# Down products with the weights stationary, and VectorE in place of TensorE for the transposes of the expert part

## What is computed

```python
# attention: q from the normalised x, k and v from ctx_1024
qh, kh = rope(q @ wq.T), rope(k @ wk.T)          # 16 heads of 64
scores = where((j <= i) & (j >= i - 64), qh @ kh.T / 8, -1e30)
x = x + tanh(g_xattn) * (softmax(scores) @ vh) @ wo.T
# experts: xt is the normalised x, 2048 tokens
shared = sum over 2 of gelu(xt @ up.T) @ down.T
probs = softmax(xt @ router_w.T)                 # 16 experts
gate = probs where among the 4 largest, else 0
routed = sum over 16 of (gelu(xt @ up.T) * gate) @ down.T   # inner width 128
x = x + tanh(g_ffn) * (shared + routed)
```

## Time and profile before

| | |
|---|---|
| median of 3 runs | 535.76 us (534.08 to 537.0) |
| the profiled execution: own time, span | 533.94 us, 532.2 us |
| granted clock of PE, mean over the span | 0.996 of full |
| attention with the last heads, up to expert 4 | 0 to 322.8 us |
| experts 4 to 71 | 322.8 to 528.6 us |
| busy share PE, DVE, ACT, POOL | 97%, 64%, 59%, 51% |

### The profile page before, as it was taken

How to read it: one execution, slowest core, us unless ns; L and a number is a source line. 1 busy time by engine, 2 the same in 40 slices (tenths; PEclk the granted TensorE clock), 3 DMA queues, 4 the chain that set the end, 5 groups by cost and what they waited for, 6 DMA issues and landing times.

```text
span 532.2 us, 13189 instructions
## 1 busy us (share of the span) xinstructions
PE 514.6 (97%) x4904; PEld 454.5 (85%) x4904; DVE 343.2 (64%) x1122; ACT 311.7 (59%) x861; POOL 273.8 (51%) x212
## 2 busy tenths in 40 slices
PE   8788999999999999999999999999999999999997
PEld 5577797789889988888889789989999989999996
DVE  5768867658675687668766647665656465645444
ACT  3367667475766567765776665664456445544442
POOL 3899998779887978897998325430100010000000
PEclk9999999999999999999999899999999999999999
DMA  8262224011031101220221047205400540046001
GB/s 264 84 174 60 67 66 139 18 36 38 10 106 36 38 1 37 57 57 22 56 58 55 3 136 249 93 1 178 181 1 1 177 182 1 1 125 234 1 1 39
DMA packets 21614, 41.03 MB, mean 77 GB/s; under 512 B 3056, under 2 KB 5360, under 8 KB 21552
## 3 DMA queue, kind: packets, MB, share of 16 engines
q1 hardware_dynamic: 21552, 40.20, 24.5%
HBM read 30.62 MB, written 2.23 MB: 62 GB/s over the span
## 4 chain that ended last, share of the span: by engine, by line
PE 74%; POOL 9%; DVE 7%; issue 5%; ACT 3%; DMA 1%; SPq 0%; DVEq 0%; POOLq 0%; ACTq 0%
PE ring L934 51%; PE psS L934 9%; PE psO L1135 4%; PE psS L1104 4%; PE psT L1116 4%; POOL arena L433 2%; POOL prob L439 2%; POOL arena L435 2%; DVE arena L717 2%; POOL arena L426 1%; PE psT L1081 1%; POOL wl L447 1%; DVE wl L788 1%; DVE arena L720 1%; DVE arena L843 1%
## 5 line engine op out<-in xcount | busy, mean ns | idle before, releaser
L934 PE MATMUL ring<-xTh,wh 128*128 128x512 f32 x272 | 111.2, 409 | 3.2 <-DVE arena L720 2.9
L934 PE MATMUL ring<-xTl,wh 128*128 128x512 f32 x272 | 106.9, 393 | 0.0
L934 PE MATMUL ring<-xTh,wl 128*128 128x512 f32 x272 | 106.9, 393 | 0.0
L934 PE MATMUL ring<-wh,oTh 128*128 128x256 f32 x272 | 78.4, 288 | 2.0 <-POOL wl L447 0.8
L934 PE MATMUL ring<-wh,oTl 128*128 128x256 f32 x272 | 76.7, 282 | 0.0
L934 PE MATMUL ring<-wl,oTh 128*128 128x256 f32 x272 | 76.4, 281 | 0.0
L439 POOL TENSOR_TENSOR prob<-prob,rinv 128x512 f32<-128x512 f32 x64 | 68.0, 1063 | 16.3 <-DVE rinv L853 16.1
L775 DVE TENSOR_TENSOR oTl<-prob,oTh 128x512 fp32r<-128x512 f32 x64 | 45.4, 710 | 43.5 <-ACT oTh L531 43.3
L531 ACT ACTIVATE oTh<-prob 128x512 fp32r<-128x512 f32 x64 | 40.4, 631 | 55.5 <-PE ring L934 25.2
L515 ACT ACTIVATE sneg<-ring 128x512 f32<-128x512 f32 x72 | 42.9, 596 | 36.8 <-PE ring L934 36.2
L767 DVE TENSOR_TENSOR prob<-sneg,arena 128x512 f32<-128x512 f32 x64 | 47.4, 740 | 26.4 <-ACT sneg L515 26.4
(11 more groups left out here) (118 smaller groups left out, 1243.7 us busy)
## 6 DMA issues: line engine op xcount, KB each, us to landing
arena<-gate_scratch SPq DMA_DIRECT2D x64, 256.0 KB, 6.3
raw<-in_e SPq DMA_DIRECT2D x18, 256.0 KB, 2.6
raw<-in_w SPq DMA_DIRECT2D x16, 256.0 KB, 3.3
arena<-arena SPq DMA_DIRECT2D x16, 256.0 KB, 3.1
arena<-arena SPq DMA_DIRECT2D x16, 192.0 KB, 3.4
out<-x SPq DMA_DIRECT2D x16, 128.0 KB, 5.8
x<-in_x SPq DMA_DIRECT2D x3, 512.0 KB, 4.1
craw<-in_ctx SPq DMA_DIRECT2D x3, 512.0 KB, 5.2
```

The source lines that it names most:

```text
L934: last = pe.matmul(out, a, b, start=start and i == 0 and j == 0, stop=stop and i == n - 1 and j == 2, skip_group_check=check)
```

## The change

- `down` keeps the weights stationary and moves the 512 tokens: 6 matmuls of 512 columns in place of 12 of 256. The sums are then turned, 2 x 128 of the 256 values on partitions and 512 tokens along them, and so are z and the output tensor (the host turns it back).
- z needs x (after attention) turned too. DVE makes this copy, x1T, in four quarters per batch ("back" at e = 9, 12, 16, 17). A quarter is four transposes from 32 partitions, 256 values each, to the four groups of 32 partitions.
- In the expert part the normalised x of the next batch is turned by DVE as well ("turn", four quarters at e = 5 to 8), in place of PE's 8 transposes; rounding is "xhi" at 9 (ACT) and the remainder "xlo" at 10 (DVE). Batch 0's is still turned by PE.
- The router's product has its weights stationary (4 matmuls of 512 columns) and DVE turns the logits (4 transposes) and the gates (4 transposes) for all batches. PE's transposes of gates go.
- "stat" goes to e = 3, "norm_a" and "norm_b" both to 4, "r", "rexp", "pick_a", "pick_b" one later (11 to 14).
- In the last heads, ACT's copy of head 58 comes before the exponential of head 60; behind it PE, ACT and DVE have another order.

```diff
-            for e, kind in ((4, "stat"), (6, "norm_a"), (7, "norm_b"), (9, "xT"), (10, "r"), (11, "rexp"),
-                            (12, "pick_a"), (13, "pick_b"), (15, "gT")):
+            for e, kind in ((3, "stat"), (4, "norm_a"), (4, "norm_b")):
+                after[b * NE + e].append((kind, B + b + 1))
+            for quarter in range(4):
+                after[b * NE + 5 + quarter].append(("turn", 4 * (b + 1) + quarter))
+            for e, kind in ((9, "xhi"), (10, "xlo"), (11, "r"), (12, "rexp"), (13, "pick_a"), (14, "pick_b"),
+                            (15, "gT")):
+                after[b * NE + e].append((kind, b + 1))
...
+            for quarter, e in enumerate((9, 12, 16, 17)):
+                after[b * NE + e].append(("back", 4 * b + quarter))
...
+            def turn(dst, src, a):
+                blocks = src[QUAD * a:QUAD * (a + 1), :, :].rearrange("p t (k c j) -> p t k c j", k=KC, c=4)
+                for c in range(4):
+                    to = dst[QUAD * c:QUAD * (c + 1), :, :].rearrange("p k (t a j) -> p t k a j", t=TT, a=4)
+                    last = dve.transpose(to[:, :, :, a, :], blocks[:, :, :, c, :])
+                return last
...
+                by_tokens = banks(("r", b))[0][0:QUAD, :].rearrange("p (t a j) -> p t a j", t=TT, a=4)
+                for a in range(4):
+                    last = dve.transpose(logits[QUAD * a:QUAD * (a + 1), :, :], by_tokens[:, :, a, :])
...
+                elif kind == "turn":
+                    b, a = divmod(n, 4)
+                    dve.wait_ge(ln_norm, B + b + 1)
+                    turn(xnT, xn, a).then_inc(xn_turned, 1)
+                elif kind == "back":
+                    b, a = divmod(n, 4)
+                    dve.wait_ge(y_out, GROUPS * (b + 1))
+                    turn(x1T, x[:, b, :, :], a).then_inc(x1_turned, 1)
...
-                for t in range(TT):
-                    half, at = t // 2, (t % 2) * D
-                    last = product(sums(b, half)[:, at:at + D],
-                                   [(hi[:, t * P:(t + 1) * P], lo[:, t * P:(t + 1) * P])],
-                                   [cols(i, D, D)], start=(e == 0 and t % 2 == 0), stop=(e == NE - 1),
-                                   check=True)
-                    last.then_inc(down_pe, 1)
+                for kc in range(KC):
+                    product(sums(b, kc), [cols(i, D + kc * P, P)], [gated_parts(n)], start=e == 0,
+                            stop=e == NE - 1, check=True).then_inc(down_pe, 1)
```

The last heads on PE, before and after:

```diff
             transpose_probs(60)
             expert(0)
+            transpose_probs(61)
             do(("y", UNITS - 2))
-            do(("gT", 0))
-            transpose_probs(61)
-            expert(1)
             values(30)
             transpose_probs(62)
+            expert(1)
+            transpose_probs(63)
             expert(2)
-            transpose_probs(63)
+            values(31)
             down(0)
-            values(31)
             expert(3)
```

More of the change, by code:

```diff
@@ L369, in store @@
             def store(b):
-                for t in range(TT):
-                    sp.wait_ge(z_out, TT * b + t + 1)
-                    sp.dma_start(out_d[b][:, t, :], x[:, b, t, :]).then_inc(out_done, 16)
+                for i in range(4):
+                    part = slice(i % 2 * (L // 2), (i % 2 + 1) * (L // 2))
+                    sp.wait_ge(z_out, 4 * b + i + 1)
+                    sp.dma_start(out_d[b][:, i // 2, part], z_of(b)[:, i // 2, part]).then_inc(out_done, 16)
             def do(job):
@@ L828, in do @@
                 elif kind == "z":
[L829 to L832, removed]
+                    dve.wait_ge(x1_turned, 4 * (n + 1))
+                    for i in range(4):
+                        kc, part = i // 2, slice(i % 2 * (L // 2), (i % 2 + 1) * (L // 2))
+                        dve.wait_ge(down_pe, KC * (NE * (n + 1) - 1) + kc + 1)
+                        dve.scalar_tensor_tensor(z_of(n)[:, kc, part], sums(n, kc)[:, part],
+                                                 tg[:, 1:2], x1T[:, kc, part],
                                                  ALU.mult, ALU.add).then_inc(z_out, 1)
@@ L1076, in do @@
                     X = side(B + n)
-                    for t in range(TT):
-                        for kc in range(KC):
-                            for part in (xTh[X], xTl[X]):
-                                last = pe.matmul(two[0][:, t * 2 * NR:(t + 1) * 2 * NR],
-                                                 part[:, kc, t * P:(t + 1) * P],
-                                                 rw_parts[:, kc, :, :].rearrange("p a e -> p (a e)"),
-                                                 start=kc == 0 and part is xTh[X],
-                                                 stop=kc == KC - 1 and part is xTl[X])
-                    last.then_inc(r_pe, 1)
-                elif kind == "gT":
-                    pe.wait_ge(r_gate, n + 1)
-                    for t in range(TT):
-                        last = pe.transpose(two[0][0:NR, t * P:(t + 1) * P], gate[:, t, :], ident[:, :])
-                    last.then_inc(gT_pe, 1)
+                    for kc in range(KC):
+                        for part in (xTh[X], xTl[X]):
+                            last = pe.matmul(two[0][0:2 * NR, :], rw_parts[:, kc, :, :].rearrange("p a e -> p (a e)"),
+                                             part[:, kc, :], start=kc == 0 and part is xTh[X],
+                                             stop=kc == KC - 1 and part is xTl[X])
+                    last.then_inc(r_pe, 1)
             def scores(c):
```

115 lines of the change are left out of this document (64 added, 51 removed).

## The result

The median after the change is 538.78 us (7 runs, 536.86 to 540.05) against 535.70 before (7 runs, 534.08 to 537.0): ratio 1.0053, interval 1.0034 to 1.0073. Slower by 3.1 us, where 1.3 us of gain was forecast; 538.8 is inside the range. The profiled execution took 540.05 us (span 538.3).

What follows compares the result with a forecast made beforehand. TensorE was taken to bound the kernel (busy 97% of the span). Terms: -9.3 off TensorE, -1.0 in the last heads, +9.0 of added waits, sum -1.3 us: median 535.76 to about 534.5, range 528.5 to 541.

Steps and rivals of the forecast that it cites:

- The step of a quarter: Expert steps with a quarter turn: VectorE's two operations and four transposes take 3.03 us against PE's new 2.78, 0.25 over.
- 5 x 0.25 = 1.2 per batch: Steps 5 to 9: PE waits 0.25 us for the remainder at each step whose VectorE time exceeds 2.78.
- 1.9 before down(4): Batch 0: moved normalising delays rounding(4), so remainder(4) ends at 332.1 where down(4) is due at 330.2: 1.9 us late.
- the 0.4 before the router: Router product waits for the lower part of x behind a gate product on VectorE: 0.4 us per batch.
- Batch 0 was to cost 3.85 us: Batch 0's added waits: 0.35 before down(3), 1.9 before down(4), 1.2 in the turning steps, 0.4 before the router.
- Rival 2: VectorE bounds the turning steps: over 0.5% slower from 0.51 us per transpose, 541.2 at 0.55; chance 0.20.
- The quarter: Four 32x256 transposes on VectorE, 0.453 us each back to back, extrapolated from the stream shuffle: 1.81 us.
- Rival 1: A quarter's transposes overlap, 0.35 us apart, 1.40 a quarter, step 2.62 under 2.78: kernel 529.2 us; chance 0.30.
- Last heads: Last attention heads up to expert 4, reordered: 0.15 + 0.44 + 0.08 + 0.3, 1.0 us gained.
- Batches 1 and 2: Costs per batch: 0.4 at down(4), 1.2 in the turning steps, 0.4 before the router product.
- End: Last batch: a quarter between gate product 71 and remainder 71 makes down(71) 1.1 us late.
- Rival 3: The slow stretch at 299 to 302 goes with the new order, 1.5 us in all: 533.0; chance 0.08.

Runs made afterwards that it cites:

- all but down: Changed kernel with the old down products (12 matmuls of 256 columns) and no turning of x1: 539.07 us, 1.0075 against the kernel before.
- router alone: Kernel before with only the new router product, logits and gates turned by VectorE, and new order of the last heads: 531.37 us, 0.9929.
- the last one without the down part: Changed kernel with POOL's wait for the gate product and early statistics, but old down products and no turning of x1: 528.24 us, 0.9856.
- the final pair: Changed kernel with POOL's wait, early statistics and earlier last quarters, 527.33 us; POOL's wait and early statistics with old down, no x1 turning, 528.24 us.
- the weight piece first: Changed kernel with ScalarE rounding its weight piece at the start of a step instead of its end: 539.86 us, 1.0091 against the kernel before.
- the three moves together: Changed kernel with weight piece first on ScalarE, statistics and normalising at steps 2, 3, 4, last batch's quarters at 9, 11, 13, 15: 531.75 us, 0.9935.

## Why the prediction was wrong, by its steps

**The step that failed** is "The step of a quarter is then 0.61 + 0.61 + 1.81 = 3.03 us" where it was used for batch 0, and with it "From then on PE waits for remainder(n) [...] 5 x 0.25 = 1.2 per batch". It takes DVE's two operations at their undisturbed spacing from expert 68, where POOL has nothing to do, and carries it to steps in which POOL subtracts weight pieces. There a step takes 4.2. The 5 x 0.25 became waits of 2.22 and 0.91, and 8 matmuls at half the clock (0.43 apart for 0.23, 1.6 us). The 1.9 before down(4) and the 0.4 before the router measured 1.45 and 1.25. Batch 0 was to cost 3.85 us against the 2.9 that PE gains, and cost 9.05 (the stretch grew by 6.15).

**Rival 2** named VectorE as the bound of the turning steps and a slower kernel; that is the outcome, but its mechanism was not: it asked for transposes of 0.51 us, and they measure 0.436. The extra microsecond lies on the operations around them.

**Right:**
- The quarter: forecast 1.81, measured 1.78, the spacing 0.45. The value came from a shuffle, an operation of another kind, which happened to be near.
- Rival 1's condition (0.35 apart) holds only when the output stays in one group of partitions. Its forecast of 529.2 stands beside 531.7 in the run that made it so.
- Last heads: 1.05 from up(0) on for 0.85 (0.15 of the 1.0 lay ahead of up(0)). Batches 1 and 2: costs of 2.25 us each (2.9 gained, 0.65 left) for the 2.0 forecast: 0.44 at down(4) for 0.4, 1.3 in the four steps behind it for 1.2, 0.55 at the router's step for 0.4. End: 1.48 us of waiting at down(71), 1.16 of it given back by earlier quarters, for 1.1.
- The waits before down(3) and down(4), 0.36 and 1.45 for 0.35 and 1.9. What I missed is what the earlier place of the statistics is worth: one step earlier gains 7.0 us once the quarters follow.
- Rival 3 didn't come: the stretch at 299 to 302 is there after too (302 to 305). It is not refuted either. The profiled executions of "all but down", "router alone" and the last one without the down part have the new order of the last heads and a clock of 1.00 there, and a longer slow stretch at 16 to 23 us instead; no run shows why.

**Sizes off.** The turning step, 3.14 us for 3.03, by the gate product that is waited out, and so the costs of batches 1 and 2 by 0.25. PE's gain of 2.9 per batch was right: a step without waits takes 2.785 us for 2.826, and the router product 0.92 (354.97 to the next up product at 355.89; the 1.08 of the chain's piece holds the length of its last matmul too) for 0.93.

**Where the expected gain is.** It is in PE's steps, 2.9 per batch. In after, waits and the slow clock take back 2.25 in each of batches 1 and 2, and 9.05 in batch 0; where most of them are taken away, 8.5 us in all remain.

**Why the down products bring so little.** In the final pair they bring at most 0.9 us, where 70 x 0.04 = 2.8 was forecast. Step by step the 0.04 is there: 17 of 18 steps of batches 1 and 2 take 2.78 or 2.79 with the new product and 2.82 or 2.83 with the old. It is spent at the router's step, 4.22 to 4.25 us with the new product and 3.76 to 3.77 with the old. The timeline of batch 2 with the down part, then without it:

```profile
444.82 1.77 DVE L757 STREAM_TRANSPOSE pT<-x 32x256 f32<-32x256 f32 x4
446.62 0.69 DVE L813 TENSOR_TENSOR oTl<-prob,oTh 128x512 fp32r<-128x512 f32 x1
...
447.83 1.22 DVE L875 TENSOR_TENSOR xTl<-pT,xTh 128x1024 fp32r<-128x1024 f32 x1
...
449.20 0.39 PE L1125 MATMUL psT<-xTh,rw_parts 128*32 128x512 f32 x1 [0.15 <-DVE xTl L875]
```

```profile
447.88 1.22 DVE L868 TENSOR_TENSOR xTl<-pT,xTh 128x1024 fp32r<-128x1024 f32 x1
...
450.16 0.40 PE L1121 MATMUL psT<-xTh,rw_parts 128*32 128x512 f32 x1
```

x1's quarter at step 9 stands in front of a remainder, a gate product and the lower part of x, and the router's first matmul starts right behind that lower part (447.83 + 1.22 = 449.05, then 449.20). Without the quarter the lower part is ready 1.06 us ahead of PE (449.10, 450.16). So 0.5 of the 0.7 gained per batch is lost there. In batch 0 the down part costs 0.5 more than it gains (52.73 against 52.24), behind the quarters at 9, 12, 16 and 17. Open is whether another place for the quarters would keep the gain; no run tried it in batches 0 to 2.

## What to carry to other kernels

The length of a VectorE operation with two SBUF inputs is that of the stretch from which it is read: look for what GpSimd does in the stretch to which it goes, and ask the trace for the longest of the line, not the mean. Slack that hides such waits is a resource; a change that spends it in one move (early statistics) and adds work in the next brings out delays that were in the kernel before. When two engines fall into step, one wait on the one with time to spare can be worth more than the change itself.

## What the hardware showed that I had not expected

- POOL's subtraction and DVE's two-input operation exclude one another: 1.71 for 0.69 when POOL starts 0.1 first, 1.82 for 1.26 when DVE does. Transposes beside POOL: 1.78 and 1.30, as alone.
- A wait of PE of 2.22 us in batch 0, with two shorter ones before it, was followed by 3.4 us at the 1.2 GHz level, 1.3 us after PE had started again. This cost 1.6 us more than the wait. It isn't certain to happen: with the weight piece first, waits of 2.65, 1.08, 2.20 and 1.13 us left the clock at 1.00, and so did 2.21 and 1.12 with the three moves together.
- A 32x256 fp32 transpose on DVE: 436 ns, 0.45 apart into another group of partitions, 0.34 apart within one (404 ns there). A transpose that reads another group of partitions than the gate product in front of it starts 0.71 behind it, one that reads the same group 0.60.
